# Softmax attentions with queries on the partitions: sums as two extra columns, outputs turned by a transpose

## The reference

```python
def _L0_xattn_ref(q, k, v, Wq, bq, Wk, bk, Wv, bv, Wo, bo):
    # q = layernorm(x); k = v = ctx; 16 heads of 8
    qh = (q @ Wq.T + bq).reshape(B, S, H, Hd).transpose(0, 2, 1, 3)
    kh, vh = ...                       # the same with Wk, bk and Wv, bv
    scores = jnp.einsum('bhqd,bhkd->bhqk', qh, kh) / jnp.sqrt(jnp.float32(Hd))
    attn = jax.nn.softmax(scores, axis=-1)
    out = jnp.einsum('bhqk,bhkd->bhqd', attn, vh)
    return out.transpose(0, 2, 1, 3).reshape(B, S, D) @ Wo.T + bo
# layer 3: the same, with q, k, v clamped, a bias added to the scores, and -10000 where mask == 0
x = x + _L0_xattn_ref(_layernorm(x, axis=-1), ctx_1024, ctx_1024, ...)
```

## Time and profile before

| | us |
|---|---|
| median of 3 runs | 569.26 (567.64 to 570.02) |
| the profiled execution | 567.78 |
| its span | 566.0 |

### The profile page before, as it was taken

How to read it: one execution, slowest core, us unless ns; L and a number is a source line. 1 busy time by engine, 2 the same in 40 slices (tenths; PEclk the granted TensorE clock), 3 DMA queues, 4 the chain that set the end, 5 groups by cost and what they waited for, 6 DMA issues and landing times.

```text
span 566.0 us, 8533 instructions
## 1 busy us (share of the span) xinstructions
PE 414.9 (73%) x3355; PEld 271.8 (48%) x3358; DVE 411.7 (73%) x867; ACT 244.2 (43%) x419; POOL 109.6 (19%) x63
## 2 busy tenths in 40 slices
PE   4997799999995773648979663799981578748115
PEld 2465376566664351314645443667761145533005
DVE  4797456475449868499778884857897899875974
ACT  3756532222223132458987531443531233333941
POOL 2100000079200000396000000200098143300000
PEclk9799799999997576768988795899995657777757
DMA  7940000000004300000000000300000000000001
GB/s 265 356 128 3 0 1 2 0 1 0 1 1 162 137 2 1 1 0 1 1 1 2 1 0 1 57 0 1 1 0 1 2 0 2 1 2 0 0 0 38
DMA packets 11068, 16.60 MB, mean 29 GB/s; under 512 B 5258, under 2 KB 9748, under 8 KB 10132
## 3 DMA queue, kind: packets, MB, share of 16 engines
q1 hardware_dynamic: 10740, 15.26, 7.9%
q10 hardware_dynamic: 288, 0.79, 0.4%
HBM read 15.52 MB, written 0.52 MB: 28 GB/s over the span
## 4 chain that ended last, share of the span: by engine, by line
PE 52%; DVE 33%; ACT 9%; issue 5%; DMA 1%; ACTq 0%; DVEq 0%
PE ps L818 6%; PE ps L823 6%; PE ps L833 6%; PE ps L1675 4%; PE ps L1684 4%; ACT arena L1468 4%; PE ps L1840 2%; PE ps L1411 2%; PE ps L1397 2%; PE ps L514 2%; PE ps L1383 2%; DVE l2buf L1761 2%; DVE arena L615 2%; PE ps L298 2%; PE ps L528 2%
## 5 line engine op out<-in xcount | busy, mean ns | idle before, releaser
L904 DVE SCALAR_TENSOR_TENSOR arena<-ps,cols,arena 128x512 f32<-128x512 f32 x40 | 29.8, 750 | 48.6 <-PE ps L823 46.6
L869 ACT ACTIVATE arena<-ps,cols 128x512 f32<-128x512 f32 x40 | 27.5, 687 | 69.5 <-PE ps L818 69.5
L1468 ACT ACTIVATE arena<-ps,const 128x512 f32<-128x512 f32 x80 | 48.8, 707 | 4.4 <-PE ps L1383 4.0
L1527 DVE TENSOR_SCALAR arena<-arena 128x512 f32<-128x512 f32 x80 | 41.8, 551 | 11.8 <-ACT arena L1468 10.5
L833 PEld LDWEIGHTS ps<-weights,arena 128*128 128x128 f32 x320 | 38.6, 192 | 8.6 <-issue 8.5
L833 PE MATMUL ps<-weights,arena 128*128 128x128 f32 x320 | 39.2, 276 | 0.2 <-DVE x_tm L893 0.2
L818 PE MATMUL ps<-h_fm,weights 128*128 128x512 f32 x80 | 38.6, 606 | 0.0
L823 PE MATMUL ps<-h_fm,weights 128*128 128x512 f32 x80 | 37.6, 592 | 0.0
L1769 POOL TENSOR_TENSOR l2buf<-l2buf,arena 128x1024 f32<-128x1024 f32 x8 | 25.4, 3215 | 47.1 <-DVE l2buf L1761 47.1
L1383 PE MATMUL ps<-l2buf,picks_b 128*128 128x256 bf16 x160 | 28.3, 307 | 7.7 <-ACT arena L1468 4.6
L573 ACT ACTIVATE arena<-arena 128x1024 f32<-128x1024 f32 x16 | 16.9, 1057 | 34.2 <-POOL arena L594 26.8
(11 more groups left out here) (311 smaller groups left out, 875.4 us busy)
## 6 DMA issues: line engine op xcount, KB each, us to landing
weights<-in_moe_w SPq DMA_DIRECT2D x2, 2048.0 KB, 10.1
weights<-in_moe_w SPq DMA_DIRECT2D x3, 1280.0 KB
l2buf<-in_picks SPq DMA_DIRECT2D x1, 1664.0 KB, 9.7
rows<-in_rows SPq DMA_DIRECT2D x1, 1216.0 KB, 13.9
x_tm<-in_x SPq DMA_DIRECT2D x2, 256.0 KB, 5.2
ctx_fm<-in_ctx_fm ACTq DMA_DIRECT2D x1, 512.0 KB, 6.0
ctx_tm<-in_ctx SPq DMA_DIRECT2D x1, 512.0 KB, 15.2
mats<-in_mats SPq DMA_DIRECT2D x1, 512.0 KB, 14.9
```

What stands on the lines that cost most here:

```text
L1468: AC.activation(hats[:, u % 2, 2 * c:2 * c + 2, :].rearrange("p r c -> p (r c)"), ps[:, m % 3, :], ACT.Abs, bias=const[:, C_NEGM:C_NEGM + ...
L1527: V.tensor_scalar(v, v, 1.0, -1.0, ALU.min, ALU.add).then_inc(hat_ok, 1)
```

## The change

- `vx` has 18 columns for each sequence and pair of heads in place of 32: 16 of values and two of ones, the first one over the first head's keys (partitions 0 to 63), the second over the second head's. POOL clears the block and writes the ones (`clear_values`).
- `weigh_values` has the turned probabilities as the stationary operand (128 keys of two heads, 64 queries) and the 18 columns as the moving one. 16 products a tile, none accumulates. The result has queries on the partitions, and in each block of 18 columns the two heads' sums stand as the last two.
- DVE takes the reciprocal over 16 sums for each token and multiplies them, spread over 8 features, with the output; the result `o_tm` is token-major in SBUF, in two buffers. PE waits for it (`ot_ready`).
- PE turns it (`turn_output`, at the end of iteration `t` for tile `t-3`), ACT copies it out of PSUM to `o_fm`, and PE multiplies with Wo at the start of iteration `t+1`. The wait on the addition of the tile before stands ahead of the turn.
- ACT spreads the values with two instructions in place of 16, one for each half of the partitions.
- Eleven late loads share the semaphore `rest_in`; each consumer waits for all eleven (`REST`).

The diff, cut to its core (what is left out replaces the waits on `rows_in`, `mats_in`, `ctxt_in`, `ffn3_in`, `mask_in`, `picks_in` and `wq8_in` by waits on `rest_in`):

```diff
@@ -129,6 +129,7 @@
         rstd = sb("rstd", [P, NT])
         kexp = sb("kexp", [P, B * 4 * S])
         v4 = sb("v4", [P, B * 8 * 32])
+        VC = 2 * HD + 2
         arena = sb("arena", [P, 10240])
         weights = sb("weights", [P, 8192])
 
@@ -169,9 +170,9 @@
             G.wait_ge(pool_chain, chained["pool"])
 
-        x_in, const_in, ctxf_in, ctxt_in = [sem("x_in0"), sem("x_in1")], sem("const_in"), sem("ctxf_in"), sem("ctxt_in")
-        rows_in, cols_in, mats_in = sem("rows_in"), sem("cols_in"), sem("mats_in")
-        rows0_in = sem("rows0_in")
+        x_in, const_in, ctxf_in, rest_in = [sem("x_in0"), sem("x_in1")], sem("const_in"), sem("ctxf_in"), sem("rest_in")
+        cols_in, rows0_in = sem("cols_in"), sem("rows0_in")
+        REST = 16 * 11
         moe0_in = sem("moe0_in")
         x_done = sem("x_done")
         hf_ready = sem("hf_ready")
@@ -214,14 +215,24 @@
             act.dma_start(ctx_fm[:], A["ctx_fm"]).then_inc(ctxf_in, 16)
 
         cleared = sem("cleared")
-        V4_CLEAR, KV_CLEAR, AB_CLEAR, V4_CLEAR_AGAIN = 1, 2, 3, 4
+        V4_CLEAR, KV_CLEAR, AB_CLEAR, V4_CLEAR_AGAIN = 3, 4, 5, 8
+
+        def clear_values(pool, cleared_so_far):
+
+            values = v4[:, 0:B * 8 * VC].rearrange("p (b m) -> p b m", m=VC)
+            G.memset(values, 0.0).then_inc(cleared, 1)
+            pool.wait_ge(cleared, cleared_so_far + 1)
+            for h2 in range(2):
+                r = slice(S * h2, S * h2 + S)
+                G.memset(values[r, :, 2 * HD + h2:2 * HD + h2 + 1], 1.0).then_inc(cleared, 1)
+            pool.wait_ge(cleared, cleared_so_far + 3)
 
         table, table_set = sb("table", [P, 2]), sem("table_set")
 
         @block.gpsimd
         def _(pool):
             G.memset(table[:], 1.0).then_inc(table_set, 1)
-            G.memset(v4[:], 0.0).then_inc(cleared, 1)
+            clear_values(pool, 0)
 
         n_sub, n_fm = [0], [0]
         stat_ready, std_ready, tr_ready = sem("var"), sem("std"), sem("hT")
@@ -320,7 +331,7 @@
 
         SCALE = 1.0 / float(np.sqrt(np.float32(HD)))
         kx = kexp[:].rearrange("p (b h k) -> p b h k", b=B, h=4)
-        vx = v4[:].rearrange("p (b c m) -> p b c m", b=B, c=8)
+        vx = v4[:, 0:B * 8 * VC].rearrange("p (b c m) -> p b c m", b=B, c=8)
         l2buf = sb("l2buf", [P, 8192])
         bqs = sb("bqs", [P, 2])
 
@@ -380,19 +391,14 @@
                 dve.wait_ge(k_sb, 2)
                 guard(k_fm[:], T, work[:, 2048:5120])
 
-            def spread_values(act, parts=range(4)):
-
-                act.wait_ge(v_sb, 5 if masked else 4)
-                act.wait_ge(cleared, V4_CLEAR_AGAIN if masked else V4_CLEAR)
-                for part in parts:
-                    h2, par = part // 2, part % 2
+            def spread_values(act, parts=range(2)):
+
+                act.wait_ge(v_sb, 5)
+                act.wait_ge(cleared, V4_CLEAR_AGAIN)
+                for h2 in parts:
                     r = slice(64 * h2, 64 * h2 + 64)
-                    c0 = (par * 2 + h2) * HD
-                    for g in range(4):
-                        src = vdup[r, g].rearrange("p b (c h d) -> p b c h d", c=4, h=4)[:, :, :, par * 2 + h2, :]
-                        dst = vx[r, 4 * g:4 * g + 4].rearrange("p b (c t) m -> p b c t m", t=2)[:, :, :, par, c0:c0 + HD]
-                        ins = AC.activation(dst, src, ACT.Copy)
-                    ins.then_inc(vx_ready, 1)
+                    src = vdup[r].rearrange("p i b (c h d) -> p (i b) c h d", c=8, h=2)[:, :, :, h2, :]
+                    AC.activation(vx[r, :, :, HD * h2:HD * h2 + HD], src, ACT.Copy).then_inc(vx_ready, 1)
 
             @block.tensor
             def _(pe):
@@ -447,13 +453,14 @@
             prob = [arena[:, 1024 * i:1024 * i + 1024] for i in range(3)]
             pT = [arena[:, 3072 + 1024 * i:4096 + 1024 * i] for i in range(2)]
             mx = arena[:, 6144:6144 + 32].rearrange("p (i h) -> p i h", i=2)
-            rb = arena[:, 6208:6208 + 128]
-            ones = const[:, C_ONES:C_ONES + 64].rearrange("p (t m) -> p t m", t=2)
+            rb = arena[:, 6208:6208 + 32].rearrange("p (i c h) -> p i c h", i=2, c=8)
+            o_tm = arena[:, 6336:6592].rearrange("p (i f) -> p i f", i=2)
+            o_at = ps[:, 6, 0:8 * VC].rearrange("p (c m) -> p c m", c=8)
             q_ps, q_sb = (s("q_ps"), s("q_sb")) if masked else (l0_q_ps, l0_q_sb)
             q_ok, mx_ready, clean = (s("q_ok"), s("max"), s("clean")) if masked else (None, None, None)
             sc_ready, sc_read, sub_ready, exp_ready = s("scores"), s("scores_read"), s("less_max"), s("exp")
             ptT_ready, pt_ready = s("probsT"), s("probsT_sb")
-            o_ready, rb_ready = s("o_ps"), s("sums")
+            o_ready, rb_ready, ot_ready, oT_ready = s("o_ps"), s("sums"), s("o_tm"), s("o_T")
             of_ready, y_ready, y_added = s("o_fm"), s("y"), s("y_added")
 
@@ -532,22 +539,28 @@
                 def weigh_values(j):
                     pe.wait_ge(pt_ready, 2 * j + 2)
                     if j == 0:
-                        pe.wait_ge(vx_ready, 4)
+                        pe.wait_ge(vx_ready, 2)
                     else:
-                        pe.wait_ge(of_ready, j)
+                        pe.wait_ge(ot_ready, j)
                     for b in range(2):
                         for c in range(8):
-                            g = c // 2
-                            PE.matmul(ps[32 * g:32 * g + 32, 6, 64 * b:64 * b + 64], vx[:, 2 * j + b, c, :],
-                                      pT[j % 2][:, 128 * c + 64 * b:128 * c + 64 * b + 64],
-                                      start=(c % 2 == 0), stop=(c % 2 == 1))
-                    for c in range(8):
-                        ins = PE.matmul(ps[32 * (c // 2):32 * (c // 2) + 32, 6, 128:256], ones[:, c % 2, :],
-                                        pT[j % 2][:, 128 * c:128 * c + 128], start=(c % 2 == 0), stop=(c % 2 == 1))
+                            ins = PE.matmul(o_at[64 * b:64 * b + 64, c, :], pT[j % 2][:, 128 * c + 64 * b:128 * c + 64 * b + 64],
+                                            vx[:, 2 * j + b, c, :], start=True, stop=True)
                     ins.then_inc(o_ready, 1)
 
+                def turn_output(j):
+                    pe.wait_ge(ot_ready, j + 1)
+                    if j >= 1:
+                        pe.wait_ge(y_added, j)
+                    PE.transpose(ps[:, 7, 128:256], o_tm[:, j % 2, :], ident).then_inc(oT_ready, 1)
+
                 scores(0)
-                for t in range(NT + 3):
+                for t in range(NT + 4):
+                    if 0 <= t - 4 < NT:
+                        j = t - 4
+                        pe.wait_ge(of_ready, j + 1)
+                        PE.matmul(ps[:, 7, 0:128], o_fm[:, j * P:j * P + P], mat(wo), start=True, stop=True)\
+                            .then_inc(y_ready, 1)
                     if t + 1 < NT:
                         scores(t + 1)
 
@@ -558,16 +571,11 @@
                     if 0 <= t - 1 < NT and masked:
                         transposes(t - 1)
                     if 0 <= t - 3 < NT:
-                        j = t - 3
-                        pe.wait_ge(of_ready, j + 1)
-                        if j >= 1:
-                            pe.wait_ge(y_added, j)
-                        PE.matmul(ps[:, 7, 0:128], o_fm[:, j * P:j * P + P], mat(wo), start=True, stop=True)\
-                            .then_inc(y_ready, 1)
+                        turn_output(t - 3)
 
             @block.scalar
             def _(act):
-                for t in range(NT + 2):
+                for t in range(NT + 4):
                     if t < NT:
                         act.wait_ge(sub_ready, t + 1)
                         AC.activation(prob[t % 3], prob[t % 3], ACT.Exp).then_inc(exp_ready, 1)
@@ -579,6 +587,10 @@
                             act.wait_ge(ptT_ready, 2 * j + k + 1)
                             AC.activation(pT[j % 2][:, 512 * k:512 * k + 512], ps[:, 4 + k, :], ACT.Copy)\
                                 .then_inc(pt_ready, 1)
+                    if 0 <= t - 3 < NT:
+                        j = t - 3
+                        act.wait_ge(oT_ready, j + 1)
+                        AC.activation(o_fm[:, j * P:j * P + P], ps[:, 7, 128:256], ACT.Copy).then_inc(of_ready, 1)
 
             if masked:
                 @block.gpsimd
@@ -639,12 +651,14 @@
                         dve.wait_ge(o_ready, j + 1)
                         if masked:
 
-                            dve_link(V.tensor_scalar(rb, ps[:, 6, 128:256], 1.0, None, ALU.max))
-                            V.reciprocal(rb, rb).then_inc(rb_ready, 1)
+                            dve_link(V.tensor_scalar(rb[:, j % 2], o_at[:, :, 2 * HD:VC], 1.0, None, ALU.max))
+                            V.reciprocal(rb[:, j % 2], rb[:, j % 2]).then_inc(rb_ready, 1)
                         else:
-                            V.reciprocal(rb, ps[:, 6, 128:256]).then_inc(rb_ready, 1)
```

(43 more changed lines are left out.)

22 lines of the change are left out of this document (10 added, 12 removed).

## The result

| | before | after |
|---|---|---|
| median | 569.64 us (567.64 to 570.60) | 617.68 us (617.29 to 617.92) |
| span of the profiled execution | 566.0 | 616.0 |
| mean granted clock | 0.819 | 0.756 |

The ratio is 1.0856 (1.083 to 1.0883): 48 us slower. The forecast was 570.8 us with a range up to 581.0, and the time lies far above that.

What follows compares the result with a forecast made beforehand. PE and DVE were taken as level in the first attention (PE the bound after), DVE as the bound in the last. 567.78 us profiled + 2.3 - 0.8 = 569.3, median 1.5 above: 570.8 us, range 565.5 to 581.

Steps and rivals of the forecast that it cites:

- Values, side by side: PE's values products: 32 records in two column halves run at once, 0.90 us per tile, else 1.79.
- rival (1): PE's values: the two halves don't run side by side, +7.2 us first attention, some +4 last, total 582; chance 0.18.
- The clock stays full in the first attention: First attention: PE keeps the full clock, iteration 4.58 us, so the stage ends 2.3 us later.
- Rival (2): Both attentions: PE, moving fewer columns and pausing, gets less full clock, +5 us first, +3 last, total 579; chance 0.20.
- DVE's part: DVE in both attentions: reciprocal over 16 columns takes 0.20 us in place of 0.96, saving 0.76 us per tile.
- The turn and the wait: PE in both attentions: turning the output and idling through ACT's copy adds 0.69 us per tile, 0.9 at half clock.
- The sum: Whole kernel: first attention +2.3 us, last -0.8, the rest nothing, giving a median of 570.8 us.
- Load and columns: PE's values: by the skill's rule load and matmul add, +0.24 us per tile, up to +4 us in all.
- Rival (3): Last attention: a busier PE keeps the full clock there, -5.8 us in place of -0.8, total 565.8; chance 0.20.
- (4): DVE's reciprocal isn't cheaper over strided columns, +2.5 us more in the last attention, total 573; chance 0.06 with others.

Runs made afterwards that it cites:

- e2: Changed kernel, each values' product moving 64 columns in place of 18, surplus results unread, order of products kept: 579.1 us.
- e12: Kernel before with all its work, plus 16 unread products per tile that load 64 columns and move 18, column halves in turn: 593.3 us.
- e13: Kernel before with all its work, plus 16 unread products per tile that load 64 columns and move 64, column halves in turn: 575.1 us.
- e6: The kernel of e3 run again (changed kernel, halves alternating, 64 moved columns): 570.05 us at the median of twelve, ratio to before 1.0004.
- e3: Changed kernel with the column halves alternating product by product and 64 moved columns in place of 18: 564.8 us in one execution.
- e10: Changed kernel with halves alternating, 64 moved columns, Wo product behind next scores, and an extra 128x256 product per tile in the last attention: ratio to before 1.0023.
- e11: Kernel before with one extra unread 128x256 product per tile in the last attention: ratio to before 0.9995.
- e8: The kernel of e1 (18 moved columns, halves alternating) with one extra unread 128x256 product per tile: 596.9 us.
- e1: Changed kernel with the two column halves alternating product by product in weigh_values, same products and sizes: 597.1 us.
- e9: Kernel before with moved columns cut from 64 to 18 (values) and 128 to 18 (sums), leaving part of the attention out: 567.8 us.

## Why the prediction was wrong, step by step

The 48 us split into two steps that the runs take away one after the other: 617.7 to 597.1 by the order of the halves (20.6), and 597.1 to 570.05 by the clock (27), where the clock was given back by moving 64 columns. The other way round it is 38.6 for the clock (617.7 to 579.1) and 9.0 for the order at the full clock.

- **Values, side by side (0.90 taken, 2.0 kept as the other end): wrong.** 3.13 us at the half clock, 1.83 at the full one (e2). The prediction let the second half's products run beside the first half's over 16 records ahead of them, and said itself that its row of 31 records does not show that reach. There was no such reach: the second half began with four records of the first left. The price of the load was right (0.056 a record, 0.058 measured), and rival (1), 582 us at an unchanged clock, is near e2's 579.1.
- **The clock stays full in the first attention: wrong, and this is the larger part.** Rival (2) named it and then priced it at "half of the 24 us", +5 and +3. In fact all of the first attention from 22 us on and all of the last went at 0.50. The argument against it, with PE busy 5.34 of 8.00 us at 1.00, measured the wrong thing: busy share. Here PE was busy 8.48 of 8.90 us at 0.50, and the kernel before had been busy 6.75 of 6.80 us at 0.50 from 24.1 to 30.9 us, a stretch that the prediction did not use. In e12 and e13 the busy share is the same to 2%, and the columns moved decide. The Trainium skill (TensorE: Matmul & The Clock Gate, Part 1) has the clock return to 1.2 GHz after an idle window, and full when busy; by that rule this kernel, hardly ever idle, would have kept the full clock in the first attention. e12 against e13 speaks against it too: busy 23.84 and 23.43 of 24.00 us, and 0.50 against 1.00.
- **The rivals were priced one by one.** (1) and (2) came together, and the half clock made the order dearer: a record costs 0.107 in place of 0.058 us, and the order is worth 20.6 us in place of 9.0. The two surcharges, 11 and 8 us, would have given 590 together, still 28 short, since rival (2) was priced for half of one attention and a little of the other.
- **DVE's part: right.** The reciprocal over 16 sums took 0.26 us (0.20 taken, 0.17 to 0.35 the bounds). DVE gave up 0.96 - 0.26 = 0.70 us a tile (0.76 taken). In the changed kernel that is worth nothing in the first attention, as DVE waited there 24 us for the values (idle before it, and its releaser):

```profile
L657 DVE RECIPROCAL arena<-ps 128x16 f32<-128x16 f32 x8 | 2.1, 257 | 24.0 <-PE ps L547 24.0
```

- **The turn and the wait: right in the first attention, too small in the last.** Copy 0.28 us (0.27 taken), start of the turn to start of the copy 0.36 (0.37; e6, 40.39 to 40.75), waking 0.05 (0.05), in all 0.69 us a tile (0.69 taken), of which the last values cover 0.07: in the chain of e6 it is 0.62. In the last attention the copy stands behind ACT's two copies of the turned probabilities, and from turn to product it is 1.13 us (e6, 483.96 to 485.09), which the prediction's one figure for both left out.
- **The sum, where the two wrong steps are undone: right, in part by luck.** e6: iteration 4.57 us (4.58), the first attention 42.8 us against 40.6, +2.2 (+2.3 forecast), the last 57.5 against 58.3, -0.7 (-0.8), the median 570.05 (570.8). These stage times are of one execution each, and e3, the same kernel, had 39.2 in the first, a larger difference than the one that was forecast. The last came out in spite of the wait above. Between and behind the attentions, where nothing was forecast, the same profile has +2.8 and -2.3. By its own terms the iteration starts at 35.5 (35.23 + 0.69 - 0.42) and not at 35.6, which takes 0.1 us off the first attention.
- **Load and columns do not add.** e2's records, all on 128 rows, with 64 moved columns, come 0.058 us apart, the price of the load alone. By the Trainium skill (TensorE: Matmul & The Clock Gate, Part 3), a load overlaps with a matmul only where the row groups differ, and the two would have added; that does not hold here.
- **Rival (3)**, the full clock in the last attention, did not come about; where more of it was bought (e10, e11) it gave nothing. **(4)** fell with the 0.26 us, since the reciprocal did get cheaper over the strided columns.

## What to carry to other kernels

Before you swap the operands of a product, compare for each record the columns loaded with the columns moved. A stretch that loads 64 and moves 18 pays three times: by the load, by the lost side-by-side run unless the column halves take turns, and by a clock that can stay at the half level for everything around it. A busy TensorE in the profile does not show that the clock is safe, so read the granted clock beside it, in the kernel before too: a half-clock stretch that ends there need not end in the changed one. When two rivals touch the same engine, price them together.

## What the runs showed of the hardware

- More work took less time twice: 38.6 us less in e2 with 46 surplus columns per product; 11 us less in the first attention of e8 with one product of 256 columns more per tile.
- A busy TensorE can be at the half clock: 6.75 of 6.80 us busy at 0.50 in the kernel before, 23.84 of 24.00 in e12, where e13 had 1.00 at 23.43.
- 32 moved columns behind loads of 64 were no better than 18 (595.2 and 597.1 us); 64 were (570.05).
- Products for two column halves ran in pairs all through where they stood next to each other in program order (e1); with 16 records of each half in a row, only the last four of one ran beside the first four of the other.
- Products with loads of 32 columns in four column groups cost so little (e9: 0.63 us for 48 records) that with their columns cut to 18 the granted clock of the last attention fell only from 0.68 to 0.61.
